# Expert lists in places of 256 and 128 rows, with the first list's transfers issued from the rows themselves

## The reference

```python
# layer 0: 8 experts, top 2 of 8, gated, and a shared expert for every token
h   = rmsnorm(x, norm2_w)
w,i = top_k(softmax(h @ router_w), 2); w = w / w.sum(-1)
x   = x + sum_j w[:, j] * (silu(h @ e_gate[i_j]) * (h @ e_up[i_j])) @ e_down[i_j]
x   = x + (silu(h @ sh_gate) * (h @ sh_up)) @ sh_down
# layer 1: 8 experts, top 2 by sigmoid score, ungated
x   = x + sum_j w[:, j] * silu(x_n @ w1[i_j]) @ w2[i_j]
```

## Time and profile before

| | |
|---|---|
| median of 3 runs | 3300.22 us |
| profiled execution | 3303.56 us |
| its span | 3301.8 us |
| mean granted TensorE clock | 0.943 |
| first mixture's stage | 1409 to 2108 us |
| second mixture's stage | 2997 to 3301.8 us |
| DMA traffic | 244.92 MB, mean 74 GB/s |

### The profile page before, as it was taken

The page is one execution under the profiler, slowest core; times in us unless marked ns, Lnnn a source line. Parts: engine busy times, 40 slices in busy tenths (PEclk is TensorE's granted clock), DMA queues, the critical chain, the costliest instruction groups (busy, mean ns, idle before and its releaser), DMA issues.

```text
span 3301.8 us, 49294 instructions
## 1 busy us (share of the span) xinstructions
PE 2775.8 (84%) x16680; PEld 1894.1 (57%) x16680; DVE 1904.4 (58%) x3429; ACT 1529.9 (46%) x2627; POOL 1460.3 (44%) x1559
## 2 busy tenths in 40 slices
PE   6888888867887888776999998699788888867998
PEld 2333333334555566533888885498455555546887
DVE  3878788875887688841222223500689888862111
ACT  4565556635675566510222221344566666642222
POOL 3666676654444577525000004500345555543444
PEclk8999999998998899988999999799899999988999
DMA  9600000000013000012566652200000100005775
GB/s 326 214 1 0 0 1 0 1 0 30 14 47 110 1 1 1 1 69 92 175 192 196 196 188 82 86 1 1 1 14 31 38 30 31 21 27 175 212 211 149
DMA packets 135984, 244.92 MB, mean 74 GB/s; under 512 B 16144, under 2 KB 107792, under 8 KB 125328
## 3 DMA queue, kind: packets, MB, share of 16 engines
q1 hardware_dynamic: 115344, 208.33, 19.4%
q0 software_dynamic: 20448, 34.11, 4.2%
HBM read 154.17 MB, written 90.05 MB: 74 GB/s over the span
## 4 chain that ended last, share of the span: by engine, by line
PE 34%; POOL 7%; DVE 6%; issue 6%; ACT 2%; POOLq 1%; another core or an unknown queue 1%; DMA 0%; SPq 0%; DVEq 0%; ACTq 0%
PE PS L2229 9%; PE PS L2187 5%; PE PS L1837 4%; PE PS L2476 4%; PE PS L2463 4%; POOL e_hs L1396 2%; POOL rows_by_expert L2118 2%; DVE e_mx L1299 1%; POOL e_qs L1399 1%; PE PS L1251 1%; POOL rows_in_place L831 1%; PE PS L1828 1%; PE PS L1194 1%; POOLq L2564 1%
## 5 line engine op out<-in xcount | busy, mean ns | idle before, releaser
L534 POOL TENSOR_TENSOR u_in<-dtx,b_rep 128x512 f32<-128x512 f32 x256 | 324.9, 1291 | 209.1 <-ACT b_rep L515 208.0
L550 DVE TENSOR_TENSOR_SCAN state<-PS,u_in 128x512 f32<-128x512 f32 x256 | 312.2, 1219 | 59.1 <-POOL u_in L534 34.9
L2250 ACT ACTIVATE d_act_b<-PS 128x256 f32<-128x256 f32 (+1 forms) x188 | 78.4, 419 | 511.7 <-PE PS L2229 432.7
L507 PE MATMUL PS<-scaled,ident 128*128 128x512 f32 x512 | 290.6, 651 | 28.6 <-DVE scaled L544 28.6
L2229 PE MATMUL PS<-d_unit_T,d_w 128*128 128x256 f32 x1248 | 284.0, 381 | 1.0 <-ACT d_unit_T L2239 1.0
L2262 DVE TENSOR_TENSOR d_hid<-d_act_b,PS 128x256 f32<-128x256 f32 (+1 forms) x188 | 87.3, 466 | 316.9 <-ACT d_act_b L2250 314.1
L1396 POOL TENSOR_TENSOR e_hs<-e_pr 128x512 f32<-128x512 f32 x128 | 162.6, 1270 | 229.3 <-ACT e_pr L1363 225.5
L2229 PEld LDWEIGHTS PS<-d_unit_T,d_w 128*128 128x128 f32 x1248 | 235.2, 191 | 32.0 <-issue 1.4
L523 ACT ACTIVATE PS<-dt,decay_rate 128x508 f32<-128x508 f32 x256 | 173.5, 686 | 132.0 <-DVE state L550 130.2
L544 DVE TENSOR_TENSOR scaled<-state,PS 128x512 f32<-128x512 f32 x256 | 169.4, 664 | 63.9 <-PE PS L488 52.2
L2136 POOL COPY d_slot_now<-d_slot 128x8 int32 x8 | 1.5, 194 | 461.1 <-DMA out_by_expert<-d_y_rows 443.3
(11 more groups left out here) (426 smaller groups left out, 6411.6 us busy)
## 6 DMA issues: line engine op xcount, KB each, us to landing
d_w<-in_d_w SPq DMA_DIRECT2D x41, 1024.0 KB, 4.9
f_w<-in_f_w SPq DMA_DIRECT2D x39, 1024.0 KB
rows_in_place<-blank SPq DMA_DIRECT2D x136, 272.0 KB, 4.5
d_w<-in_d_w SPq DMA_DIRECT2D x41, 512.0 KB, 3.9
f_unit_rows<-rows_in_place SPq DMA_DIRECT2D x39, 272.0 KB, 5.1
rows_by_expert<-zeros SPq DMA_DIRECT2D x39, 256.0 KB, 2.8
d_unit_rows<-rows_by_expert SPq DMA_DIRECT2D x39, 256.0 KB, 4.0
out_by_expert<-d_y_rows SPq DMA_DIRECT2D x39, 256.0 KB, 4.0
```

The costliest lines, as they stand in the source:

```text
L507: nc.tensor.matmul(YB[:, c], ident[:], scaled[:, (KD * n + c) % RC], start=False, stop=n == NS - 1).then_inc(m_y, 1)
L534: nc.gpsimd.tensor_tensor(u_in[:, k % RU], dtx[:, p, c], b_rep[:, n % RB], ALU.mult).then_inc(m_u, 1)
L550: nc.vector.tensor_tensor_scan(state[:, k % 2], DECAY[:, k % RD], u_in[:, k % RU], 0.0, ALU.mult, ALU.add).then_inc(m_h, 1)
```

## The change

It alters how long the lists are and how the first one is written and read.

Places. An expert's rows are now padded to a multiple of 128, and the places are of two kinds: FULL = 31 places of 256 rows and SINGLE = 9 of 128, 40 in all and 71 tiles of 128 in place of 78. An expert with an odd number of tiles takes one single place. Places that the routing leaves unused are worked off all the same, as before. The tables get a second count per expert (count - 128), boundaries of the full and the single places (17 values), and a list of the places' positions (`unit_no`), which POOL writes with 40 one-column memsets.

In the first mixture the order is `slot_order`: one full place, then nine loop turns of [full, full, single, full], then three full places written out. In the second, `unit_plan` puts a single place behind every three or four full ones; the last place is a single. In a single place the gate/up passes have 128 columns, there are two transposes in place of four and half of the down passes; the weights are loaded as for a full place. The repeated load of the shared weights goes to ring slot 1.

Transfers of the first list. `stage_group`, `staged_rows`, `slot_now`, `share_now` and `mark` are gone. POOL writes its 64 scatters one after another as soon as `placed` says that the slots are there (which VectorE now tells before it makes the table of the places), with rows and slots read from where they are. The gathers of the read-back read `slot` itself, and are written out; they still wait for `combined`. `collect_group` reads `share` itself.

```diff
+def split_units(groups):
+    halves = (2 * groups * GT - 8) // 128 + 8
+    single = 8 + halves % 2
+    return (halves - single) // 2, single
+
+def slot_order(groups):
+    full, single = split_units(groups)
+    order = [(2, 0)]
+    for n in range(single):
+        order += [(2, 3 * n + 1), (2, 3 * n + 2), (1, n), (2, 3 * n + 3)]
+    return order + [(2, n) for n in range(3 * single + 1, full)]
...
@@ router_vector, before the slots
-            link(V.tensor_tensor(filled[:], until[:, :, TILES - 1:TILES].broadcast_to([128, E, FILLS]), ...))
+            link(V.tensor_copy(count[:, 0], until[:, :, TILES - 1]))
+            link(V.tensor_scalar(count[:, 1], until[:, :, TILES - 1], -128.0, None, ALU.add))
+            link(V.tensor_tensor(filled[:], count.rearrange("p z e -> p (z e)").unsqueeze(2).broadcast_to([128, 2 * E, FILLS]), ...))
...
+            link(V.tensor_scalar(starts[:, 0:1], ends[:, E - 1:E], float(2 * FULL), None, ALU.max))
+            link(V.tensor_tensor_scan(ends[:, E:], ones_e[:], starts[:], 0.0, ALU.mult, ALU.add))
...
+            link(V.tensor_tensor(moved[:], place[:], over_n(2), ALU.is_ge))
+            link(V.tensor_tensor(moved[:], moved[:], over_n(1), ALU.mult))
...
             link(V.tensor_copy(slot.rearrange("p g s j -> p (g s) j"), slot_f[:]))
+            dve.sem_inc(placed, 1)
+            dve.wait_ge(numbered, 1)
...
@@ staging and the transfers
-        def stage_group(dve, turn, p):
-            g = 2 * turn + p
-            after(dve, in_list[p], 16 * 2 * GS * turn)
-            nc.vector.tensor_copy(staged_rows[:, p], rows_full[:, g])
-            nc.vector.tensor_copy(slot_now[:, p], slot[:, g]).then_inc(staged, 1)
...
@@ run
+                unit(eng, j + (SHN + 1), *LST(j + 1, 0), LST(j, 1), "half")
+                unit(eng, j + (SHN + 2), *LST(j + 2, 1, "half"), LST(j + 1, 0), "list")
+                unit(eng, j + (SHN + 3), *LST(j + 3, 0), LST(j + 2, 1, "half"), "list")
...
@@ list_experts
-                        step = nc.tensor.matmul(UB(f), w_up[:, u % RING, c, f * 128:f * 128 + 128], xT[:, u % 2, c], start=c == 0, stop=c == KD - 1)
+                        step = nc.tensor.matmul(UB(f)[:, 0:wide(u)], w_up[:, u % RING, c, f * 128:f * 128 + 128], xT[:, u % 2, c, 0:wide(u)], start=c == 0, stop=c == KD - 1)
...
-                for k in range(UT):
+                for k in range(tiles[u]):
                     nc.gpsimd.indirect_dma_start(tokens_of, bass.IndirectOffsetOnAxis(token[:, u % RING, k:k + 1], 0), y[:, u % 2, k], None,
                                                  bounds_check=NG * GT - 1, oob_is_err=False, compute_op=ALU.add).then_inc(added, 16)
```

More of the change, by code:

```diff
@@ L2176, in output_tensor @@
         def output_tensor(pe, v, kind, at, p, r):
-            if kind == "list":
+            if kind != "shared":
                 wait_ring(pe, w_dn, at, r)
             pe.wait_ge(hidden, v * FC + FC)
-            for h in range(2):
+            parts, tiles = (1, 1) if kind == "half" else (2, width[kind] // 2 // 128)
+            for h in range(parts):
                 pe.wait_ge(taken, 2 * v + h + 1)
                 out_h = DB(h, kind)
-                tiles = width[kind] // 2 // 128
                 for q in range(tiles):
@@ L2264, in unit_vector @@
                     output_vector(dve, u - 1, *before)
-                if kind == "shared" and again is None and (f == 1 or f == 3 and ahead):
-                    stage_group(dve, u + f // 2, 1 - f // 2)
                 if again and f % 2 == 0:
@@ L2270, in output_vector @@
         def output_vector(dve, v, kind, at, p, r):
-            if kind == "list":
+            if kind != "shared":
                 turns = 16 * (at // 2) if isinstance(at, int) else 8 * (at - p)
                 dve.wait_ge(y_out[p], turns + 16)
-            for h in range(2):
-                dve.wait_ge(down, 2 * v + (h + 3))
+            parts = 1 if kind == "half" else 2
+            for h in range(parts):
+                dve.wait_ge(down, 2 * v + (h + 5 - parts))
                 o = DB(h, kind)
@@ L2301, in run @@
-            before = LST(UNITS - 1, 0)
-            for g in range(SHN, NG if SHN else 0):
-                now = SHR(g, 1 - g % 2)
-                unit(eng, UNITS + g, *now, before, None, again=g - SHN)
-                before = now
-            output(eng, (UNITS + NG if SHN else UNITS) - 1, *before)
-        def load_rows(sp, j, jp):
+            SHR = lambda g, gp, r=0: ("shared", g, gp, r)
+            LST = lambda j, jp, kind="list": (kind, j, jp, ring_of(jp))
+            unit(eng, 0, *SHR(0, 0), None, "shared")
@@ L2310, in load_rows @@
+            for j in range(4 * SINGLE + 1, UNITS):
+                unit(eng, SHN + j, *LST(j, j % 2), LST(j - 1, 1 - j % 2), "list" if j + 1 < UNITS else None)
+            last = LST(UNITS - 1, (UNITS - 1) % 2)
+            for g in range(SHN, NG):
+                now = SHR(g, (UNITS + g) % 2, AGAIN)
+                unit(eng, UNITS + g, *now, last, None, again=g - SHN)
+                last = now
+            output(eng, UNITS + NG - 1, *last)
+        def load_rows(sp, j, jp, at, tiles):
             after(sp, turned, j - 1)
-            sp.dma_start(unit_rows[:, jp], list_units[:, j]).then_inc(row_in[jp], 16)
+            sp.dma_start(unit_rows[:, jp, 0:tiles], list_rows[:, bass.ds(at, tiles)]).then_inc(row_in[jp], 16)
@@ L2403, in pool @@
         def pool(pl):
+            for u, half in enumerate(half_of(NG)):
+                step = nc.gpsimd.memset(unit_no[:, u:u + 1], float(half))
+            step.then_inc(numbered, 1)
             rows["pool"](pl)
@@ L2459, in output_tensor @@
             pe.wait_ge(hidden, FC * u + FC)
-            for r in range(UT):
-                after(pe, mixed, UT * (u - 1) + r + 1)
+            for r in range(tiles[u]):
+                after(pe, mixed, had(u, r))
                 for f in range(FC):
@@ L2468, in tensor @@
             turn_rows(pe, 0)
-            for u in range(UNITS):
+            for u in range(SLOTS):
                 for f in range(FC):
```

343 lines of the change are left out of this document (183 added, 160 removed).

## The result

| | before | after |
|---|---|---|
| median of 5 runs | 3300.29 us (3293.65 to 3305.23) | 3323.04 us (3316.91 to 3327.48) |
| profiled execution, its span | 3303.56, 3301.8 us | 3323.04, 3321.2 us |
| ratio | | 1.0069, 95% interval 1.0055 to 1.0082 |

A forecast was written before the change was run, and what follows sets the result against it. Both lists were taken as bound by TensorE's passes. The terms -28.4 - 17.4 - 1.9 - 5 - 4 = -56.7 us gave 3244 us for the median; the forecast's own range was 3230 to 3258, the full range 3222 to 3284.

The forecast's parts named there:

- The list's transfers: Start of the first list: 64 scatters without staging, TensorE's 17.4 us of waits unchanged, list starts earlier: -5 us.
- Rival A: First list's start: POOL's unbroken run holds TensorE's signals to its end, list 34 us later; 3283 us, chance 0.17.
- The POOL side: First list's scatters: 64 without a pause end at 1542 to 1544, which would allow -12.5 to -14.6 us.
- The second list: Second list in places of 256 and 128: -17.4 us, and -1.9 at its end; nothing charged for the scatter-add chain.
- C2: Second list, rival set in an experiment: the add chain is too long by itself, above 290 us; no chance given.
- The first list: First list in places of 256 and 128: 36.9 us gained less 8.5 of stalls, -28.4 us (-20 to -37).
- the stalls: First list's half places: TensorE waits for late hidden rows, 0.95 us a half place (0 to 1.9).
- rival D: Both lists: a half place costs a full one's time because it loads all weights; 3307 us, chance 0.04.
- The rule of the Trainium skill: TensorE: weight loads overlap matmuls only when row groups differ, so 128-column passes would stay near 0.21 us.
- rival C: Both lists: 128-column passes cost what 256 columns cost, for their weight loads; 3272 us, chance 0.05.
- The read-back: Read-back's 8 groups: each loses POOL's slot copy, the mark, hand-overs and VectorE's share copy: -4 us (-2 to -5).
- rival E: Both lists: stalls at the 18 halves drop TensorE's clock from 2.4 to 1.2 GHz, +83; 3327 us, chance 0.04.

The follow-up runs named there:

- e10: The changed kernel unaltered, run a third time, in session 3 where signals were held: 3322.65 us.
- e6: The kernel before, unaltered, run again for its trace in session 2, where nothing was held: 3277.7 us.
- e8: The changed kernel without the second list's weight loads behind the first three, scatter-adds kept: the second list's passes took 267.9 us.
- e5: The changed kernel unaltered, run once more in session 2, where nothing was held: 3251.68 us, ratio 0.9939 to the kernel before.
- e12: The kernel before, unaltered, run a third time, in session 3 where signals were held: 3291.39 us.
- e1: The changed kernel with POOL waiting before each scatter group for VectorE's hidden rows, session 1, nothing held: 3253.16 us, ratio 0.9953.
- e9: The changed kernel with POOL's waits for VectorE between scatter groups and the second list's 128-row places last, session 3: 3253.13 us, ratio 0.9876.
- e11: The changed kernel with POOL waiting before each scatter group for VectorE's hidden rows, session 3, signals held: 3292.68 us.
- e15: The changed kernel with a POOL operation between any two groups of 8 scatters, session 5, where signals were held: 3286.34 us.
- e2: The changed kernel with a POOL operation between any two groups of 8 scatters, session 1, nothing held: 3266.2 us, ratio 0.9988.
- e3: The changed kernel with the second list's nine 128-row places behind its 31 full ones, session 1: 3217.43 us, ratio 0.9846.

## Why the prediction was wrong, by its own steps

**The list's transfers (-5 forecast, +38.9 measured).** The step that failed reads "The number of scatters is the same, so I take the same 17.4 us, spread otherwise". The 17.4 us were a property of runs of 24 and less. In one run of 64 the waits grew to 61.8 us in one piece (30.3, 17.3 and 4.0 us in e10). Rival A had the mechanism, though in e10 signals also came through inside the run, and 34 us for its price; I gave it 0.17 because events arrived within the run of 24. That was a weak reason: the runs that the trace shows were all shorter than the one to come. The POOL side was right: the last scatter at 1543.0, forecast 1542 to 1544.

**The second list (-17.4 and -1.9 forecast, +12.7 and +2.7 measured).** The failing step: "8.3 us from end to end, less the part of the wait that was TensorE's own pace. ... I charge nothing (bound: 2 us a half)". Before, the chain's own cycle was 1.85 us to the last add's issue, 4.36 to its landing and 0.86 to the next issue: 7.1 us of the 7.33 between places. TensorE set the pace with under 0.3 us to spare, and VectorE waited 14.3 us for landings even then. I took a busy TensorE for proof of slack elsewhere. TensorE's side was sized well: 269.0 us without adds against 290.0 in e6 is -21, forecast -17.4. What I had at nothing is that landings get longer. With those of before, 31 x 7.07 + 9 x 5.22 gives an estimate of 266 us for the chain, under TensorE's 269; with the 5.26 us measured behind full places and 4.55 behind halves it is 296 us, near the 301.4 of the passes. Why they get longer behind halves is argued, not shown; that the weight loads lengthen them is shown by e8, where C2 (above 290 us) falls. The bound of 2 us a half was missed too: within session 2 it is 305.2 - 269.0 = 36.2 us, 4.0 a half.

**The first list (-28.4 forecast, -35.3 measured)** was right in kind. 9 halves at 5.94 in place of 6.45 save 8 x 10.80 - 9 x 5.94 = 32.9 us: the stalls were 0.44 us each, not 0.95. The other 2.4 us are the list's start, and not foreseen: from the first place's transposes to the second's it took 14.58 us before, behind a wait of 9.62 us and with a granted clock of 0.57 in the first 7.3 us, and 12.17 us now, where TensorE comes straight from the shared units at 1.00. The weights kept up, as calculated, so the prediction's rival D is out. The rule of the Trainium skill that is quoted there doesn't hold for these passes, and rival C falls with it: 128 columns with a load of their own pass in 0.11 us.

**The read-back (-4 forecast, -1.4 measured)**: -2.0 us between e6 and e5, where nothing is held; in session 3 it went the other way, from 121.9 us in e12 to 127.2 in e10. The late signals, not POOL's copies, set it: 105 to 109 us without a hold, 119 to 127 with it.

**The clock (rival E)** did not fall in the first list (1.00). It fell to 0.56 in the long wait and to 0.96 in the second list, after waits that had other causes.

With the forecast of the first list, and the other four terms as measured, the sum is -28.4 + 38.9 - 1.4 + 12.7 + 2.7 = +24.5, against +19.4 of the spans. Where nothing is held the change gains 20 us (3272.08 to 3251.68) and not 56.7, so the hold alone doesn't account for the miss: the second list's step fails there too.

## What to carry to other kernels

An engine that is busy all of the time doesn't show that the next chain has slack: before shortening its work, add up the other chain's own cycle, issue to landing to next issue, and compare it with the period, and ask whether landings stay as short when transfers come closer; a chain of 7.1 us under a period of 7.33 looks like no bound at all. When work of uneven sizes must pass a chain with a fixed cost per item, put the small items together at the end (here 31.6 us). Small copies and waits between indirect transfers may be what keeps other engines' signals flowing. A wait on the receivers' own progress (e1, e9, e11) breaks the run only when they fall behind, and cost nothing that showed where nothing was held; a fixed pause after every eight broke it too, at about 11 us. And measure in more than one session.

## What the runs showed of the hardware

- Unbroken runs of POOL's indirect transfers held TensorE's completion signals in sessions 3 and 5 and in the first comparison, and not at all in sessions 1, 2 and 4, for one and the same kernel (the changed one: 1.0069 of the kernel before in one, 0.9939 in another). Signals within the first ten or so scatters came on time; what was held came about 2.6 us after a run of 24 and 9.2 us after one of 64, but in e10 in part inside the run, 23.6 and 1.2 us before its end. Each session was wholly of one kind. The record gives the same chip number, 2, for session 1 without a hold and session 5 with one; if that is the same chip, the hold doesn't go with the chip. What it goes with, and why it comes about, stays open.
- With a pause of 1.8 us of POOL after every eighth scatter no hold was seen (e15, one execution); it costs about 11 us where there is none (the list starts at 1551.7 in e2 and 1538.3 in e1, whose scatters also begin 2.8 us earlier).
- The last scatter-add (128 rows) of a full place landed 3.8 us after its issue without weight loads beside it (e8), 4.6 us with them when the full places stand together (e3), and 5.3 us on average, up to 8.8, with halves between them (the changed kernel).
